# Another hand-out of an image's work over the 64 steps of a five-engine pipeline

## The reference, cut to what matters

```python
x = x + L0(_gn(x))     # outlook attention, stride 2
x = x + L1(_gn(x))     # 3x3 depthwise convolution with the signs of the weights
```

```python
a = jax.nn.softmax(a * scale, axis=-1)
out = jnp.einsum('bnpqk,bnpkd->bnpqd', a, v_un)
folded = folded.at[:, ii, jj, :].add(out)
return folded[:, PAD:PAD + hh, PAD:PAD + ww, :] @ W_o + b_o
```

## Time and profile before

| | |
|---|---|
| median of 3 runs | 5449.22 us (5446.7 to 5451.9) |
| the profiled execution's own time | 5428.43 us |
| span of its core | 5426.3 us |
| mean granted TensorE clock over the span | 0.83 of full speed |
| busy share of the span | PE 79%, DVE 77%, POOL 62%, ACT 36% |
| products | 2048 of L607, 64 per image |

### The profile page before, as it was taken

One profiled execution on the slowest core, in us unless ns is written; L12 is line 12 of the kernel. 1 busy time (PEld: TensorE's weight loads), 2 busy tenths in 40 slices (PEclk: granted clock), 3 DMA queues, 4 the chain that ended last, 5 costly groups with the idle time before them and its releaser, 6 DMA issues.

```text
span 5426.3 us, 58203 instructions
## 1 busy us (share of the span) xinstructions
PE 4262.7 (79%) x13632; PEld 2144.5 (40%) x13632; DVE 4194.5 (77%) x4747; ACT 1968.1 (36%) x2881; POOL 3365.6 (62%) x3628
## 2 busy tenths in 40 slices
PE   4877888777887788878778877788778887777874
PEld 2434444344443344433444433344334444344432
DVE  5677777788777877777777778777777777788787
ACT  3324333343343244332433333334324433343331
POOL 5766665666666656666666666566565666666662
PEclk7988887888888888887888888888888888888886
DMA  1110111111111101111011111111110111111110
GB/s 37 36 45 20 44 42 29 45 27 36 44 30 43 43 21 44 38 34 45 21 42 42 29 45 31 33 42 33 40 45 20 44 40 31 45 27 36 44 29 21
DMA packets 222997, 195.55 MB, mean 36 GB/s; under 512 B 114600, under 2 KB 215816, under 8 KB 222824
## 3 DMA queue, kind: packets, MB, share of 16 engines
q1 hardware_dynamic: 194152, 155.50, 12.9%
q10 hardware_dynamic: 28672, 38.55, 2.4%
HBM read 39.22 MB, written 38.54 MB: 14 GB/s over the span
## 4 chain that ended last, share of the span: by engine, by line
POOL 52%; issue 40%; DVE 3%; PE 3%; POOLq 1%; ACT 1%; DVEq 0%; SPq 0%; DMA 0%; ACTq 0%; PEldq 0%; PEld 0%
POOL prod L369 21%; POOL att L351 10%; POOL att L357 9%; POOL part L362 8%; POOL pc L338 2%; PE acc L762 2%; DVE strip L657 1%; POOLq L249 1%; DVE prod L607 1%; PE bc L742 1%; POOL pooled L344 1%; POOL rstd L378 1%; DVEq L253 0%; DVE top L637 0%; DVE top L633 0%
## 5 line engine op out<-in xcount | busy, mean ns | idle before, releaser
L762 PE MATMUL acc<-prod,wo 96*96 96x392 f32 x5312 | 2568.4, 586 | 376.3 <-DVE X L621 365.1
L607 DVE TENSOR_TENSOR prod<-bc,VAL 96x784 f32<-96x784 f32 x2048 | 1960.9, 963 | 907.6 <-PE bc L742 831.9
L369 POOL TENSOR_TENSOR prod<-prod 96x392 f32<-96x392 f32 x1440 | 1456.3, 1014 | 1442.3 <-DVE prod L607 1437.8
L742 PE MATMUL bc<-stack,sel 96*96 96x392 f16 x4608 | 1320.7, 382 | 646.5 <-DVE prod L607 625.5
L762 PEld LDWEIGHTS acc<-prod,wo 96*96 96x96 f32 x5312 | 993.4, 192 | 937.3 <-DVE X L621 527.8
L742 PEld LDWEIGHTS bc<-stack,sel 96*96 96x96 f16 x4608 | 575.8, 139 | 1604.1 <-DVE prod L607 1062.0
L657 DVE SCALAR_TENSOR_TENSOR strip<-XP,sg,strip 96x448 f32<-96x448 f32 x1568 | 1062.6, 678 | 158.0 <-ACT strip L540 138.6
L351 POOL TENSOR_TENSOR att<-att,top 108x420 f32<-108x420 f32 (+1 forms) x576 | 590.5, 1043 | 164.7 <-DVE top L633 164.7
L439 ACT ACTIVATE att<-side,ba 108x420 f32<-108x420 f32 (+1 forms) x576 | 340.2, 596 | 909.3 <-PE side L709 892.4
L357 POOL TENSOR_TENSOR att<-att,top 108x420 f32<-108x420 f32 (+1 forms) x576 | 591.0, 1045 | 66.9 <-ACT top L473 66.9
L432 ACT ACTIVATE VAL<-side 96x392 f32<-96x392 f32 (+1 forms) x256 | 126.5, 513 | 1362.0 <-DVE prod L607 1219.3
(11 more groups left out here) (56 smaller groups left out, 2184.1 us busy)
## 6 DMA issues: line engine op xcount, KB each, us to landing
stack<-part SPq DMA_DIRECT2D x192, 275.3 KB
stack<-part SPq DMA_DIRECT2D x192, 256.9 KB
tok_in<-in_x SPq DMA_DIRECT2D x32, 1176.0 KB, 7.8
out<-tok_out ACTq DMA_DIRECT2D x224, 168.0 KB, 2.1
stack<-part SPq DMA_DIRECT2D x192, 30.5 KB
stack<-part SPq DMA_DIRECT2D x192, 28.5 KB
X<-in_L_conv_W_a SPq DMA_DIRECT2D x1, 364.5 KB
ACC<-select SPq DMA_DIRECT2D x1, 144.0 KB
```

Source lines behind the costliest of these rows:

```text
L369: nc.gpsimd.tensor_tensor(p[:, 0, :], p[:, 0, :], p[:, 1, :], ALU.add).then_inc(pre_added, 1)
L607: nc.vector.tensor_tensor(prod[:, g % PRODUCTS, :, :].rearrange("c a (i j) -> c a i j", j=WIN), b, v, ALU.mult).then_inc(prod_ready, 1)
L742: last = nc.tensor.matmul(bc[g % 2][0:CH, a, 0:UNIT], sel[:, which, :], stack[h][:, qi, ki * TAPS + kj, si:si + HALF, sj:sj + WIN], start= ...
L762: last = nc.tensor.matmul(acc[0:CH, 0:UNIT], wo[:, :], prod[:, g % PRODUCTS, a, :], start=first, stop=s == LAST[c] and (g in PRE or t == 2 ...
```

## The change

Only the table `AT` changes, and with it which engine adds some pairs. Almost every entry gets another step. What is computed, the buffers, the waits in the code and the order of pieces within one kind stay. The list `"not pre"` grows from 15 entries to 27; four of the new list (12, 27, 44, 59) were never in `PRE`, so `PRE` goes from 45 steps to 60 - 23 = 37. For the eight others PE does two multiplications where it did one.

```diff
 AT = {
-    "not pre": (0, 3, 8, 9, 10, 14, 15, 16, 22, 28, 33, 39, 46, 51, 54),
-    V: ((27, 30, 33, 33), (62, 63, 65, 67)),
-    LOG: ((19, 19, 21, 21, 21, 22, 22, 23, 23), (39, 39, 42, 43, 48, 48, 48, 51, 53)),
-    IN: (5, 7, 7, 8, 9, 10, 10),
-    OUT: (19, 25, 31, 37, 43, 49, 55),
-    GA: (13, 5),
-    GB: (17, 10),
-    "gn scale": (15, 9),
-    "squares": (13, 7),
-    "pooled": (9, 34),
-    "pool normed": (17, 37),
-    MAX: ((24, 24, 27, 27), (56, 57, 57, 58)),
-    SUB: ((26, 27, 28, 29, 30, 30, 32, 33, 34), (58, 59, 59, 62, 64, 64, 64, 65, 66)),
-    EXP: ((33, 36, 37), (64, 65, 67)),
-    SUM: ((36, 37, 38, 39), (70, 71, 73, 73)),
-    INV: ((41, 43), (74, 75)),
-    UP: ((42,), (76,)),
-    MUL: ((44, 44, 45, 46, 47, 47, 48, 48, 49), (75, 76, 77, 78, 78, 79, 82, 83, 84)),
-    HIGH: ((47, 48, 49), (81, 83, 86)),
-    LOW: ((48, 49, 51, 51, 52, 52, 53, 54, 54), (81, 81, 84, 84, 85, 87, 88, 88, 88)),
-    "normed": (18, 33),
+    "not pre": (11, 12, 14, 24, 25, 26, 27, 29, 31, 32, 33, 34, 35, 36, 37, 43, 44, 45, 48, 51, 53, 54, 55, 56, 59, 61, 63),
+    V: ((28, 34, 34, 35), (58, 64, 65, 78)),
+    LOG: ((19, 19, 20, 20, 21, 22, 22, 23, 23), (34, 35, 36, 36, 37, 38, 42, 47, 51)),
+    IN: (6, 8, 8, 9, 10, 12, 13),
+    OUT: (26, 26, 38, 40, 52, 54, 58),
+    GA: (14, 6),
+    GB: (17, 9),
+    "gn scale": (16, 8),
+    "squares": (15, 7),
+    "pooled": (14, 26),
+    "pool normed": (17, 31),
+    MAX: ((24, 25, 26, 26), (54, 56, 56, 58)),
+    SUB: ((27, 27, 28, 29, 30, 31, 33, 35, 36), (58, 58, 59, 60, 61, 61, 62, 63, 63)),
+    EXP: ((27, 28, 29), (57, 61, 68)),
+    SUM: ((34, 34, 35, 37), (67, 68, 72, 72)),
+    INV: ((36, 38), (71, 73)),
+    UP: ((39,), (73,)),
+    MUL: ((36, 39, 40, 43, 43, 44, 45, 47, 47), (73, 73, 74, 74, 75, 75, 78, 79, 82)),
+    HIGH: ((42, 45, 52), (81, 83, 85)),
+    LOW: ((47, 48, 49, 51, 51, 51, 55, 55, 55), (82, 85, 85, 85, 86, 86, 87, 88, 88)),
+    "normed": (25, 39),
     "start x1": 4,
-    "start acc": 1,
-    "rimmed": 10,
-    "centred": (12, 18, 24, 30, 36, 42, 48),
-    "taps": (13, 13, 14, 15, 15, 16, 17, 17, 19, 19, 20, 21, 21, 22, 23, 23, 25, 25, 26, 27, 27, 28, 29, 29, 31, 31, 32, 33, 33, 34, 35, 35, 37, 37, 38, 39, 39, 40, 41, 41, 43, 43, 44, 45, 45, 46, 47, 47, 49, 49, 50, 51, 51, 52, 53, 53),
+    "start acc": 4,
+    "rimmed": 9,
+    "centred": (11, 18, 22, 27, 38, 40, 44),
+    "taps": (12, 14, 15, 15, 15, 16, 17, 17, 19, 19, 19, 20, 20, 21, 22, 22, 23, 23, 27, 28, 29, 30, 30, 30, 32, 33, 35, 35, 36, 37, 37, 37, 38, 39, 39, 40, 40, 41, 43, 45, 46, 47, 47, 47, 47, 48, 48, 49, 50, 50, 51, 52, 53, 53, 54, 55),
 }
```

## The result

The changed kernel takes 4600.28 us (median of 4 runs, 4592.55 to 4607.69), the kernel before beside it 5450.56; the ratio is 0.8438, 95% interval 0.8418 to 0.8458. Forecast were 4915 us with a range of 4690 to 5190. So the direction was right, and the gain was 850 us instead of 534: the range did not hold it. The time is the one of the rival "the clock stays open" (4580).

A forecast was written before the change was run, and what follows sets the result against it. DVE's 130.1 us per image plus its idle time, nearly all waits for broadcasts, bounds the kernel; idle falls from 36.3 to 19 (8 full-clock, 11 half-clock), so 5428.4 - 534 = 4894 profiled, 4915 us as median, range 4690 to 5190.

The forecast's parts named there:

- the clock stays open: Rival: gaps of 2 us no longer close PE's clock; idle 8 us per image, 4580 us in all; chance 0.12.
- I take 11 of these 15, since the traced clock fell at nearly every such place: Half-clock idle per image at 31 to 33 (3), 47 to 49 (3), 59 to 2 (5), 14 to 16 (4).
- new wait at tap 0, step 12: Stretch 7 to 12: ACT's chain to the early centre tap takes 5.0 us against DVE's 2.6; new wait 2.4.
- the old order would leave about 18 of its 36: Old order's idle per image at full clock; the other half came from class ends and short steps at half clock.
- So its 130.1 stay: DVE's busy time per image: same instructions in another order, so 130.1 us stay and only the idle 36.3 can change.
- the class ends: Taps behind class additions cover them: about 3.9 us saved at 30, 2.1 at 54; stretch 47 to 53 idles 0, not 6.6.
- the earlier softmax: Half 0's softmax moves up; the sum's 3.2 us wait for the last exponential at step 36 shrinks to about 0.3.
- The full-clock part: Idle per image with the clock at full: 0.3 + 2.4 + 1.5 + 3.6, about 8 us.
- The price lies under DVE's work: Eight pair additions moved to PE add 5.3 us at full clock, 10.6 at half, covered where DVE's step is longer.
- POOL was not what DVE waited for, so the saving is nothing by itself: Taking eight pair additions off POOL frees 8.1 us per image there but by itself gains nothing.
- Cover for the DMA: SP's issues and landing end about 5 us before broadcast 32: hidden, the narrowest cover; each us beyond costs one per image.
- PE is the bound: Rival: PE can't use over 74% of its granted clock, so 176 us per image, 5730 us in all; chance 0.07.

The follow-up runs named there:

- a_warm: New order plus unneeded filler multiplications on PE, 25 at 5 steps and 22 at 3 class ends per image; 4554.71 us, 0.8373 of old.
- a_pre8b: New order with eight pair additions given back from PE to POOL (steps 24, 25, 51, 53, 54, 55, 56, 61); 4736.03 us, 0.8705 of old.
- a_bare30: New order with the three taps of step 30 moved ahead to step 29, leaving that class end uncovered; 4686.56 us, 0.8612 of old.
- a_bare47: New order with the four taps of step 47 moved ahead to step 46, leaving that class end uncovered; 4831.03 us, 0.8873 of old.
- b_cover30: Old order with the two taps of step 29 moved behind the class end at step 30; 5350.38 us, 0.9833 of old.
- b_newpre2: Old order with only the whole new "not pre" list, eight more multiplications on PE per image; 5413.93 us, 0.9934 of old.
- a_best2: New order with a_warm's filler, first tap at step 14, pair addition 10 on PE, last two taps behind class end 62, last result transpose at 63; 4550.24 us.
- a_unroll2: New order with two image bodies in each turn of the hardware loop, 15 turns for 30; 4679.20 us, 0.8607 of old.
- a_best3: a_best2 with the load of the next image's input issued only after PE's value piece of step 64; 4503.98 us, 0.8282 of old.
- b_warm: Old order plus 39 unneeded filler multiplications on PE per image at 3 steps (29, 38, 60); 5429.33 us, 0.9985 of old.

## Why the prediction was right in direction and wrong in size

The step that failed is the sum's sentence "I take 11 of these 15, since the traced clock fell at nearly every such place". The runs showed 1.1 to 1.4 us in place of the 11. The terms of the sum against the new order, us per image:

| term | forecast | measured |
|---|---|---|
| wait of the sum for the exponential | 0.3 | 0 in the loop |
| new wait at tap 0, step 12 | 2.4 | 2.04 |
| centre tap 1, step 19 | 1.5 | 0.8 |
| product 63 | 1.3 | 1.33 |
| products 1 and 2 | 2.3 | 0.4 |
| turn of the loop, ahead of product 0 | none | 2.9 |
| step 15 | in the next row | 0.7 |
| half clock | 11 | 1.1 to 1.4 (a_warm); at 30 to 33 1.3, at 14 to 16, 47 to 49 and 59 to 2 none |
| idle in all | 19 | 10.3 |

- *Half clock, mis-sized.* I charged it at four places. At three of them, 14 to 16, 47 to 49 and 59 to 2, the clock does not fall at all in the new order: it is 0.98 to 1.00 there. It falls at 11 and 12 (0.92, 0.78), at 28 to 32 (0.67 to 0.80), at 40 and 41 (0.81, 0.75) and at 54 and 55 (0.81, 0.52), but these falls lie under taps, maxima and sums of DVE or, at 12, under its wait for ACT. Only at 30 to 33 does one cost anything, 1.3 us, where I had 3: the cover that I had just counted at full clock (2.0 us of taps for a chain of 1.2) also hides most of the chain at half clock. Why the clock stays up at 59 to 2 is open: in a_pre8b, with eight multiplications less for PE and a longer turn of the loop, it falls to 0.60 at step 2, and no run separates the two. The same mistake stood in "the old order would leave about 18 of its 36": with the clock at 0.96 it leaves 30.8.
- *DVE's own time.* "So its 130.1 stay" fails by 1.5 us per image, 44 of the 315 us that the forecast is off. The work stays (138.2 us of durations), but the busy time counts the overlap of two records once, and with fewer waits more of them overlap.
- *Right:* the class ends (30 and 47 by a_bare30, a_bare47 and b_cover30; 54 only by its stretch, which idles 0 instead of 2.1), the earlier softmax (wait 3.2 to 0), the centre taps, the new waits at 12 and 19 with their chains, and fill and tail unchanged. The full-clock part, 8 us, was measured as 9.1 in a_warm, but that is luck: the short steps 1 and 2 cost 2 us less, and the turn of the loop 3 more.
- *Eight multiplications for PE.* "The price lies under DVE's work" held: b_newpre2 is not slower, but 0.7% faster. The sentence "POOL was not what DVE waited for, so the saving is nothing by itself" fails for the new order, where giving them back costs 121 to 136 us, in part by the clock (46 come back with filler) and in part by the load at the turn.
- *Cover for the DMA.* The broadcast's transfers stayed hidden as forecast. The transfer that did cost was the input load, which no instruction waits for at that point: in the shorter image it came to lie across DVE's branch, 0.7 us per image of what the change would have given, and 2.1 with a_best2.
- *Rivals.* "The clock stays open" gave the time to 20 us, and half of the mechanism: the clock stays open at three of the four places where I charged it, and where it does fall (0.95 in the loop, not 1; opening it gains 0.8 to 1.0% in a_warm) it is covered. That its time is so near is in part luck, since it has neither the turn of the loop nor DVE's shorter busy time. "PE is the bound" is out: with DVE idle for 10.3 us an image, PE uses 108 of 138.9 x 0.95 = 132 us granted, 82%, above the 78% at which it would decide. Image 31, where I took 5 us off, is 5.7 longer (idle 16.1 to 21.7); no run looks at it.

## What to carry to other kernels

Put independent work of the bounding engine right behind each hand-over to another engine, and not ahead of it: ahead, it also idles the engine that has the chain next, and a_bare47 shows both in 7.2 us. Price a lower clock only where the chain is bare, after the cover is subtracted. And when an image gets shorter, look at what now falls on the loop's branch: a transfer that no instruction waits for yet can still stop an engine there.

## What the runs showed of the hardware that was not expected

- DVE stops at each turn of the loop for 2.7 us at least, ACT, POOL and SP for 0.2; at the loop's exit, which does not jump, it is 0.52 in the old and the new order. In a_unroll2, with a body of two images, ACT needs 2.4 to 2.7 and PE idles 3.0 to 4.5 at the turn as well.
- In the trace's transfer records an 8 KB packet of an instruction queue starts 0.9 to 1.2 us after DVE's branch in a_best3 and in 28 of the 29 turns of the old order, 0.9 to 1.9 us after it in the new one, and 2.3 to 3.1 in a_best2, there just as the packets of the input load end; DVE goes on 1.8 to 2.2 us after that packet starts. In a_unroll2 a second instruction queue moved 155 packets of 16 KB, where it moved 11 in the new order. So the stop is most likely instructions being fetched, and the load delays the fetch. That the load delays DVE is shown by a_best3; that it is through this packet is read from the records alone.
- More work on an engine can make the kernel faster: 157 useless multiplications per image of the old order gained 180 us, 47 in the new one 35 to 46. Filler that is followed by another gap gained nothing sure (b_warm, 0.9966 to 1.0004).
